# Attention and expert layer on one core: exponential's factor by columns, weight maxima by TensorE, own block for first keys

## Chip, cores and metric

One Trainium2 chip, one of its cores. The time is that of one execution of the program on the device, in microseconds; of several runs the median is given. Profiles are single executions. The program is written for the five engines by hand: TensorE (PE; its weight loads are PEld), VectorE (DVE), ScalarE (ACT), GpSimd (POOL), and SyncE (SP), which issues most DMAs. Each engine works its own queue in order, and they wait for each other on semaphores.

## The reference, cut

```python
x = L0_attn_hidden_states                                   # (4, 1024, 256) f32
x = x + attention(_layernorm(x), Wqa, Wqb, Wkva, Wkvb, Wo)
x = x + experts(_layernorm(x), gate_w, w_gate_up, w_down, shared_gate_up, shared_down)

# attention: 16 heads of 128 (64 plain + 64 rotary), values 128, from a latent of 64
q = ((x @ Wqa) @ Wqb).reshape(b, s, 16, 128)
kv_comp = x @ Wkva;  c_kv, k_pe = kv_comp[..., :64], kv_comp[..., 64:]
q_pe, k_pe = rope(q_pe), rope(k_pe)                         # k_pe is shared by the heads
k_nope, v = split((c_kv @ Wkvb), (64, 128))
scores = einsum('bhqd,bhkd->bhqk', q_full, k_full) * 128 ** -0.5
probs = softmax(where(causal, scores, finfo.min))
out = einsum('bhqk,bhkd->bqhd', probs, v).reshape(b, s, 2048) @ Wo

# experts: top 2 of 16 (softmax of logits), inner size 176, and a shared expert of 352
y = sum over the two chosen e of w_e * (silu(x @ gate_e) * (x @ up_e)) @ down_e
y = y + (silu(x @ g_s) * (x @ u_s)) @ shared_down
```

## The kernel before

**Arithmetic.** Matrices are multiplied in float16 with every operand split into a high and a low part (`hi`, `lo`), three products each. Weights are scaled so that their largest magnitude is `WMAX`. For that `first_weights` takes maxima per partition on VectorE (`largest`, L1336), GpSimd spreads the maxima of the first two columns across partitions with `partition_all_reduce` (L1941; a second one for four more columns at L1978), and `scales` computes the factors. `SPLITS` lists the weights to be split; ScalarE makes the high part (`hi_parts`, L1066), VectorE the low part (`lo_parts`, L1347). The first five entries (`FIRST`) are wanted by the first projections; `wsd` is split at the end of tile 0, `wout`, `wsg` and `wr` in tile 1. K's up-projection is folded into the query weights and V's into the output weights at the start (`wq_made`, `fold_out`), so scores and values work on the latent of 64.

**Tiles.** The 4096 tokens are 32 tiles of 128 (`NT`), eight in a batch (`TB`). Tile t with i = t % 8 has (i+1) x 128 keys. It is worked in units of `GROUP[i]` = 8, 4, 2, 2, 1, 1, 1, 1 heads, so 2, 4, 8, 8, 16, 16, 16, 16 units. For each unit: scores into four banks of PSUM `s_ps` (TensorE), largest score per row (VectorE, `maxima` or `half_maxima`: `smax`), its product with the negative factor `f_natt` (`nmax`, the bias of the exponential), exponential (ScalarE, L1166 and L1171), transposition of the probabilities (TensorE, L853), high part of it (ScalarE, L1039), low part (VectorE, `prob_lo`, L1625), product with the values (TensorE). Scores run two units ahead, exponentials one. `half_maxima` serves tiles with i = 1, 2, 3 (product at L1607) and 6, 7 (L1604); `maxima` serves i = 4, 5 (product at L1585) and i = 0. Between units, at places fixed in the tables `FIRST_TILE` to `LONG`, lie side jobs: projections of tile t+2, output projection of t-1, gates and shared expert of t-2. They share a PSUM bank. GpSimd makes the normalisations (`norm`), the rotation (`rope`; its products are L1885, L1890, L1891), low parts and scatters. From about 1420 us on, the experts' part follows, which the change doesn't touch.

**Order on SP.** Keys and queries of tile n are turned by DMA transposition (`turn_keys`, `turn_queries`, L479, L469) in the section of tile n-2. `kT` holds the keys of one batch; the first two tiles of a batch may be turned into it only when all scores of the batch before are made (L478). `turn_output` turns the outputs; for tile 0 it waits for the split of `wsd`, whose raw weights lie in the buffer `oT`.

**Opening.** TensorE runs `busy` products on a block of ones, then the weight products, `fold_out(0, 1)`, the projections of tiles 0 and 1, the rest of `fold_out`, and `first_scores(0)`. VectorE waits for nine constant tables, converts them, takes the means of the first three tiles of x (each after the normalisation before it, `normed`), then the weight maxima. ScalarE copies the eight pieces of the folded query weights (`wq_copied`) which the eight `amax_q` maxima read.

## Time and profile before

| | us |
|---|---|
| median of 3 runs (lowest, highest) | 1678.92 (1678.5, 1679.54) |
| the profiled execution, its time | 1665.37 |
| its span, first to last instruction | 1663.3 |
| TensorE busy | 1491.1 |
| VectorE busy | 1317.2 |
| ScalarE busy | 1029.8 |
| GpSimd busy | 988.8 |
| mean granted TensorE clock, of full | 0.976 |

Busy times are of one profiled execution. A busy share is a mean over stages with different limits; what ends TensorE's idle time in a stage has to be read from its waits. The profiled execution is shorter than the median of the runs by 13.5 us.

### The profile page before, as it was taken

What the parts mean: (1) busy time and instruction counts of PE and PEld (TensorE: products, weight loads), DVE (VectorE), ACT (ScalarE), POOL (GpSimd) and SP (SyncE); (2) the same over time, 40 slices, a digit from 0 to 9 for tenths busy, and PEclk for the clock granted to TensorE, in tenths of its full rate; (3) what the DMA queues carried; (4) which work ended last, traced back from release to release, by engine and by line L of the source; (5) the groups of instructions that cost most, each with busy time, mean ns of one, the idle gap of its engine ahead of it and who ended that gap; (6) DMA issues with size and microseconds to landing.
All of it is one profiled execution on the core that took longest, in us unless ns stands there. A gap on an engine that the chain in (4) does not pass through costs nothing.

```text
span 1663.3 us, 45076 instructions
## 1 busy us (share of the span) xinstructions
PE 1491.1 (90%) x16403; PEld 1081.6 (65%) x16404; DVE 1317.2 (79%) x2990; ACT 1029.8 (62%) x2342; POOL 988.8 (59%) x1597
## 2 busy tenths in 40 slices
PE   7679999999889999998899999988999998889990
PEld 2356767777666676676667766766677766666660
DVE  2687898887789888887888888878878898565556
ACT  2466666665666666766666666666666676556660
POOL 3267756543687663675878687758686572443440
PEclk9799999999999999999999999999999999999995
DMA  6348832122443312224342223143431211456318
GB/s 188 58 109 191 132 79 55 29 62 57 81 105 75 73 33 60 62 39 94 78 95 60 51 61 65 33 93 82 80 73 42 62 30 35 114 165 201 126 39 306
DMA packets 329879, 144.42 MB, mean 87 GB/s; under 512 B 277347, under 2 KB 320390, under 8 KB 329673
## 3 DMA queue, kind: packets, MB, share of 16 engines
q1 hardware_dynamic: 304592, 105.41, 29.3%
q10 hardware_dynamic: 18168, 19.41, 3.9%
q0 software_dynamic: 6912, 16.83, 3.0%
q8 instruction: 132, 2.16, 0.5%
q14 instruction: 75, 0.61, 0.1%
HBM read 47.04 MB, written 29.53 MB: 46 GB/s over the span
## 4 chain that ended last, share of the span: by engine, by line
PE 53%; DVE 25%; ACT 7%; issue 5%; DMA 4%; SPq 1%; POOL 1%; ACTq 0%; DVEq 0%; POOLq 0%
PE of_ps L683 22%; PE s_ps L683 19%; PE t_ps L853 11%; DVE pT L1625 7%; DVE smax L1596 3%; ACT pT L1039 2%; DVE smax L1600 2%; DVE smax L1578 2%; DVE nmax L1607 2%; DMA qT<-work 1%; ACT work L1039 1%; ACT probs L1171 1%; DVE nmax L1604 1%; DVE work L1430 1%; DVE o_sb L1459 1%
## 5 line engine op out<-in xcount | busy, mean ns | idle before, releaser
L683 PE MATMUL s_ps<-kT,qT 128*128 128x512 f16 (+3 forms) x2304 | 491.4, 328 | 11.3 <-DMA qT<-work 5.5
L1039 ACT CAST pT<-t_ps 128x512 f16<-128x512 f32 (+3 forms) x688 | 354.5, 515 | 236.9 <-PE t_ps L853 235.2
L1625 DVE TENSOR_TENSOR pT<-t_ps,pT 128x512 f16<-128x512 f32 (+3 forms) x688 | 408.8, 597 | 112.3 <-ACT pT L1039 109.5
L853 PE MATMUL t_ps<-id,probs 128*128 128x128 f32 x2304 | 380.3, 280 | 44.6 <-DVE pT L1625 34.5
L853 PEld LDWEIGHTS t_ps<-id,probs 128*128 128x128 f32 x2304 | 255.3, 141 | 143.7 <-issue 97.9
L683 PEld LDWEIGHTS s_ps<-kT,qT 128*128 128x128 f16 x2304 | 218.8, 99 | 78.6 <-DMA qT<-work 6.0
L1166 ACT ACTIVATE probs<-s_ps,nmax,fac 128x640 f32<-128x640 f32 (+3 forms) x256 | 269.0, 1051 | 0.6
L683 PEld LDWEIGHTS of_ps<-ckv,pT 128*128 128x128 f16 x6912 | 241.7, 98 | 40.7 <-DVE o_sb L1459 9.1
L683 PE MATMUL of_ps<-ckv,pT 128*128 128x64 f16 x6912 | 258.4, 193 | 6.7 <-DVE o_sb L1459 6.3
L683 PE MATMUL of_ps<-weights,xT 128*128 128x512 f16 (+1 forms) x936 | 199.9, 350 | 34.7 <-DVE weights L1347 16.4
L1901 POOL TENSOR_TENSOR os_<-o_sb,os_ 128x512 f16<-128x512 f32 x60 | 70.3, 1172 | 162.2 <-ACT os_ L1039 153.3
L1596 DVE TENSOR_REDUCE smax<-s_ps 128x1 f32<-128x512 f32 (+1 forms) x256 | 157.4, 647 | 3.2 <-PE s_ps L683 2.5
L683 PEld LDWEIGHTS of_ps<-weights,xT 128*128 128x128 f16 x936 | 78.5, 99 | 109.8 <-DVE weights L1347 17.1
L1171 ACT ACTIVATE probs<-s_ps,nmax,fac 128x256 f32<-128x256 f32 (+3 forms) x224 | 144.3, 651 | 3.5 <-DVE nmax L1607 3.5
L1578 DVE TENSOR_REDUCE smax<-s_ps 128x1 f32<-128x768 f32 (+2 forms) x136 | 122.6, 901 | 16.2 <-PE s_ps L683 16.1
L683 PE MATMUL s_ps<-maskbf,idbf 128*128 128x128 bf16 x512 | 113.4, 222 | 0.0
L1885 POOL TENSOR_TENSOR work<-work,sin_sb 128x544 f32<-128x544 f32 x60 | 96.4, 1607 | 24.3 <-ACT work L1039 21.7
L1600 DVE TENSOR_REDUCE smax<-s_ps 128x1 f32<-128x512 f32 (+2 forms) x160 | 95.2, 627 | 2.6 <-PE s_ps L683 2.4
L683 PE MATMUL of_ps<-weights,oT 128*128 128x256 f16 x768 | 89.1, 273 | 2.1 <-DVE work L1430 2.1
L683 PE MATMUL s_ps<-wd_sb,work 88*128 (+1 forms) x480 | 72.0, 279 | 17.2 <-DVE work L1773 9.7
L683 PE MATMUL s_ps<-wgu_sb,pT 128*128 (+1 forms) x480 | 86.0, 315 | 0.1
L683 PEld LDWEIGHTS of_ps<-weights,oT 128*128 128x128 f16 x768 | 73.6, 98 | 12.2 <-DVE work L1430 2.5
(227 smaller groups left out, 2434.9 us busy)
## 6 DMA issues: line engine op xcount, KB each, us to landing
wgu_sb<-wgu ACTq DMA_DIRECT2D x8, 704.0 KB, 4.6
work<-lists SPq DMA_DIRECT2D x40, 128.5 KB, 2.2
qT<-lists SPq DMA_DIRECT2D x40, 128.5 KB, 2.2
x_sb<-x SPq DMA_DIRECT2D x32, 128.0 KB, 2.4
x<-x SPq DMA_DIRECT2D x32, 128.0 KB, 2.3
dense<-den SPq DMA_DIRECT2D x32, 128.0 KB, 2.7
weights<-dense ACTq DMA_DIRECT2D x1, 4096.0 KB
qT<-y_exp SPq DMA_DIRECT2D x16, 256.0 KB, 6.9
```

Of the source, the lines that this page charges most:

```text
L683: return pe_.matmul(o, a, b, start=start, stop=stop)
L853: last = pe_.transpose(t_ps[:, h, c * P:(c + 1) * P], probs[:, u % 2, g * L + j * P:g * L + (j + 1) * P], id32[:, :])
L1039: return act.copy(o, i)
L1166: act.activation(probs[:, par, 0:L], s_flat[:, 1024 * par:1024 * par + L], ACT.Exp, bias=nmax[:, par, 0:1], scale=f_att, accum_out=ssum[:, ...
L1171: last = act.activation(probs[:, par, g * L:(g + 1) * L], s_flat[:, base:base + L], ACT.Exp, bias=nmax[:, par, g:g + 1], scale=f_att, accu ...
L1578: dve.tensor_reduce(smax[:, par, 0:G], view, AX_X, ALU.max).then_inc(s.maxs, 1)
L1596: last = dve.tensor_reduce(smax[:, par, h:h + 1], bank[:, 0:(j1 - j0) * P], AX_X, ALU.max)
L1600: last = dve.tensor_reduce(smax[:, par, h * n:(h + 1) * n], view, AX_X, ALU.max)
L1607: last = dve.tensor_scalar(nmax[:, par, 0:G], smax[:, par, 0:G], f_natt, None, ALU.mult)
L1625: dve.tensor_tensor(pT[:, u % 2, 1, h, 0:w], t_ps[:, h, 0:w], pT[:, u % 2, 0, h, 0:w], ALU.subtract).then_inc(s.lo_p, 1)
L1885: st_.do(pool.tensor_tensor(rot2[:, :, k:ROPE:2], pe_of(n)[:, :, 1 - k:ROPE:2], sin_b, ALU.mult))
L1901: pool.tensor_tensor(os_[:, 1, :], o_sb[:, :], os_[:, 0, :], ALU.subtract).then_inc(s.lo_o, 1)
```

## The change

It has these parts. The factor `nmax` is computed for one column per instruction, and where there are two half maxima by a TENSOR_SCALAR with two pointer operands in place of a SCALAR_TENSOR_TENSOR. The first spreading of the weight maxima goes through TensorE: transposition of two columns, maximum over the row, a diagonal of the two values, product with ones. Keys of a batch's first tile get a block of their own, `k0T`; they are turned a second time into `kT` for the later tiles. Identity products (`busy_id`) are put behind the spreading (10) and ahead of the first scores (14). VectorE takes the first mean before the constants, the second and third among the weight maxima. The late splits are cut into six and put behind units of tiles 1 and 2, and the raw `wsd` moves to another buffer.

```diff
--- before.py
+++ after.py
...
+        k0T = sb("k0T", [P, 2, P], F16)
...
+        r_wsd, at = cut(ga, at, 3, D)
...
-        r_wsd, _ = cut(oT[:, :, :, :].rearrange("p a k n -> p (a k n)").bitcast(F32), 0, 3, D)
...
+            *((r_out[:, a:a + 4], wout[:, 0, a:a + 4], wout[:, 1, a:a + 4], P, A_O) for a in (0, 4)),
             (r_wsd, wsd_sb[:, 0], wsd_sb[:, 1], P, A_SD),
-            (r_out, wout[:, 0], wout[:, 1], P, A_O),
-            (r_wsg, wsg_sb[:, 0], wsg_sb[:, 1], P, A_SG),
+            *((r_wsg[:, k], wsg_sb[:, 0, k], wsg_sb[:, 1, k], P, A_SG) for k in range(KD)),
             (r_wr, wr_sb[:, 0], wr_sb[:, 1], P, A_R),
...
+    SPLIT_AT = {at_: slice(FIRST + a, FIRST + b)
+        for at_, (a, b) in {(1, 0): (0, 1), (1, 1): (1, 2), (1, 2): (2, 3), (1, 3): (3, 4), (2, 0): (4, 6)}.items()}
...
             def turn_keys(n):
                 sp.wait_ge(s.rope_done, n + 1)
                 i = n % TB
-                if i < 2 and has(n - 2):
-                    last = n - i - 1
-                    sp.wait_ge(s.s_made, 2 * (unit_of(last, units(last) - 1) + 1))
-                sp.dma_start_transpose(kT[:, :, i * P:(i + 1) * P], ...).then_inc(k_in[n % KS], 16)
+                if i == 0 and has(n - TB):
+                    sp.wait_ge(s.s_made, 2 * unit_of(n - TB + 1, 0))
+                if i == 1 and has(n - 2):
+                    sp.wait_ge(s.s_made, 2 * unit_of(n - 1, 0))
+                dst = kT[:, :, i * P:(i + 1) * P] if i else k0T[:, :, :]
+                sp.dma_start_transpose(dst, ...).then_inc(k_in[n % KS], 16)
+            def turn_first_keys(n):
+                if has(n - 1):
+                    sp.wait_ge(s.s_made, 2 * unit_of(n, 0))
+                sp.dma_start_transpose(kT[:, :, 0:P], ...).then_inc(k0_in, 16)
...
             def turn_output(p, hh):
                 sp.wait_ge(s.lo_o, 2 * p + hh + 1)
-                if p == 0 and hh == 0:
-                    sp.wait_ge(s.lo_made, FIRST + 1)
...
                 if i == TB - 1 and has(t + 1):
                     turn_keys(t + 1)
+                    turn_first_keys(t + 1)
...
             for n in range(2):
                 turn_keys(n)
                 turn_queries(n)
+            turn_first_keys(0)
...
+            def busy_id(o, count):
+                for _ in range(count):
+                    mm(o, id16[:, :], id16[:, :].unsqueeze(1).broadcast_to([P, 4, P]), True, True)
...
                     pe_.wait_ge(k_in[t % KS], 16 * (t // KS + 1))
+                    if i == 1:
+                        pe_.wait_ge(k0_in, 16 * (t // TB + 1))
...
-                                  kT[:, b, c0:c1], a + b == 0, a == 1 and c1 < L)
+                                  kT[:, b, c0:c1] if i else k0T[:, b, c0:c1], a + b == 0, a == 1 and c1 < L)
...
             fold_out(0, 1)
+            pe_.wait_ge(s.amax_ready, 1)
+            pe_.transpose(f_ps[0:2, 0:P], amax[:, 0:2], id32[:, :]).then_inc(s.amax_turned, 1)
+            pe_.wait_ge(s.amax_spread, 1)
+            mm(f_ps[:, P:P + 2], ones_r[:, :], diag_w[:, :], True, True).then_inc(s.amax_turned, 1)
+            busy_id(s_ps[:, 1, :], 10)
...
             fold_out(1, H // 4)
+            busy_id(s_ps[:, 3, :], 14)
             first_scores(0)
...
+                if (t, k) == (2, 0):
+                    act.wait_ge(s.lo_made, FIRST + 3)
...
                     if (t, k) == (1, 0):
-                        hi_parts(SPLITS[FIRST + 1:FIRST + 2])
-                    if (t, k) == (1, 1):
-                        hi_parts(SPLITS[FIRST + 2:])
+                        act.wait_ge(s.scales, 2)
+                    if (t, k) in SPLIT_AT:
+                        hi_parts(SPLITS[SPLIT_AT[t, k]])
                     expert_loads(t, k)
                 side(t, units(t), 0)
-                if t == 0:
-                    act.wait_ge(s.scales, 2)
-                    hi_parts(SPLITS[FIRST:FIRST + 1])
...
                 for n in range(8):
+                    if n in (1, 4):
+                        means(1 if n == 1 else 2, -1)
                     dve.wait_ge(s.wq_copied, n + 1)
...
-                dve.wait_ge(s.amax_reduced, 1)
-                scales(slice(0, 2))
+                dve.wait_ge(s.amax_turned, 1)
+                link(dve.tensor_reduce(top_w[:, :], f_ps[0:2, 0:P], AX_X, ALU.max))
+                dve.tensor_scalar(diag_w[:, :], id32[0:2, 0:2], top_w[:, 0:1], None, ALU.mult).then_inc(s.amax_spread, 1)
+                dve.wait_ge(s.amax_turned, 2)
+                scales(slice(0, 2), f_ps[:, P:P + 2])
...
                 if G == 1:
-                    last = dve.scalar_tensor_tensor(nmax[:, par, 0:1], smax[:, par, 0:1], smax[:, par, 1:2], f_natt, ALU.max,
-                                                    ALU.mult)
+                    last = dve.tensor_scalar(nmax[:, par, 0:1], smax[:, par, 0:1], smax[:, par, 1:2], f_natt, ALU.max, ALU.mult)
                 else:
-                    last = dve.tensor_scalar(nmax[:, par, 0:G], smax[:, par, 0:G], f_natt, None, ALU.mult)
+                    for g in range(G):
+                        last = dve.tensor_scalar(nmax[:, par, g:g + 1], smax[:, par, g:g + 1], f_natt, None, ALU.mult)
...
             means(0, -1)
-            means(1, -1)
-            means(2, -1)
+            constants()
             first_weights()
...
-                    if (t, k) == (1, 0):
-                        lo_parts(FIRST + 1, FIRST + 2)
-                    if (t, k) == (1, 1):
-                        lo_parts(FIRST + 2, len(SPLITS))
+                    if (t, k) in SPLIT_AT:
+                        lo_parts(SPLIT_AT[t, k].start, SPLIT_AT[t, k].stop)
...
-                if t == 0:
-                    lo_parts(FIRST, FIRST + 1)
...
-            pool.wait_ge(s.amax_ready, 1)
-            pool.partition_all_reduce(amax_all[:, 0:2], amax[:, 0:2], P, bass.bass_isa.ReduceOp.max).then_inc(s.amax_reduced, 1)
```

## Rows read from the trace of the kernel before

**Rows 1.** Page, busy time of TensorE and VectorE with share of the span
```profile
PE 1491.1 (90%) x16403; PEld 1081.6 (65%) x16404; DVE 1317.2 (79%) x2990; ACT 1029.8 (62%) x2342; POOL 988.8 (59%) x1597
```

**Rows 2.** Waits of TensorE, 125 to 1420 us: total us, times, longest us
```profile
PE t_ps L853 <- DVE pT L1625: 31.4, 63, 1.5
...
PE s_ps L683 <- DMA kT<-ks_sb: 5.0, 3, 2.2
```

**Rows 3.** VectorE's groups by form: count | busy us, mean ns | idle before
```profile
L1604 DVE SCALAR_TENSOR_TENSOR nmax<-smax,fac 128x1 f32<-128x1 f32 x128 | 49.6, 387 | 4.5
L1607 DVE TENSOR_SCALAR nmax<-smax,fac 128x2 f32<-128x2 f32 x64 | 44.0, 687 | 2.3
L1585 DVE TENSOR_SCALAR nmax<-smax,fac 128x1 f32<-128x1 f32 x128 | 27.4, 214 | 4.5
```

**Rows 4.** Timeline 479 to 484 (tile 10): start us, us, engine, instruction [idle before]
```profile
480.11 2.49 POOL L1891 TENSOR_TENSOR work<-work 128x1088 f32<-128x1088 f32 x1
...
480.29 2.34 DVE L1607 TENSOR_SCALAR nmax<-smax,fac 128x2 f32<-128x2 f32 x1
...
483.23 0.52 PE L853 MATMUL t_ps<-id,probs 128*128 128x128 f32 x3 [1.49 <-DVE pT L1625]
```

**Rows 5.** Timeline 257 to 260 (tile 5), GpSimd and VectorE
```profile
258.27 2.50 POOL L1891 TENSOR_TENSOR work<-work 128x1088 f32<-128x1088 f32 x1
...
258.39 0.21 DVE L1585 TENSOR_SCALAR nmax<-smax,fac 128x1 f32<-128x1 f32 x1
```

**Rows 6.** Timeline 79 to 81, VectorE, two independent small instructions
```profile
80.02 0.14 DVE L1385 TENSOR_SCALAR fac<-wamp 128x1 f32<-128x1 f32 x1
80.08 0.20 DVE L1386 TENSOR_SCALAR fac<-wamp 128x1 f32<-128x1 f32 x1
```

**Rows 7.** Timeline of the opening, all engines (SPq issues DMAs)
```profile
25.25 0.43 DVE L1479 BATCH_NORM_STATS2 ln_st<-x_sb 128x6 f32<-128x256 f32 x1 [6.55 <-POOLq L675]
...
33.17 0.27 DVE L1354 MEMSET oT<- 32x256 f32 x1
...
36.29 4.83 DVE L1336 TENSOR_REDUCE amax_q<-work 128x1 f32<-128x512 f32 x8
...
45.74 0.17 DVE L1339 TENSOR_SCALAR amax_all<-amax_all 128x2 f32<-128x2 f32 x1 [4.37 <-POOL amax_all L1941]
...
49.59 2.74 PE L683 MATMUL of_ps<-weights,xT 128*128 128x512 f16 x6 [1.02 <-DVE weights L1347]
...
71.36 0.50 PE L683 MATMUL s_ps<-kT,qT 128*128 128x128 f16 x3 [5.52 <-DMA qT<-work]
...
72.67 4.97 SPq L469 DMA_TRANSPOSE qT<-pT  x1
...
74.13 0.39 POOL L1978 PARTITION_ALL_REDUCE amax_all<-amax  x1 [8.16 <-DVEq L1379]
```

**Rows 8.** DMA issues at the start, and issues by tensor: KB each, us to landing
```profile
4.37 1.06 SPq L417 DMA_DIRECT2D x_sb<-x  x2
...
11.14 0.46 ACTq L1043 DMA_DIRECT2D wd_sb<-gateT  x1
...
x_sb<-x SPq DMA_DIRECT2D x3, 128.0 KB, 9.4
...
wd_sb<-gateT ACTq DMA_DIRECT2D x1, 16.0 KB, 12.3
```

**Rows 9.** Windows: us, busy (instructions) of PE, PEld, DVE, ACT, POOL, PEclk, DMA share, GB/s
```profile
47.00:51.00 4.00, 2.24 (x10) 1.15 (x11) 3.24 (x4) 4.00 (x5) 0.00 (x0) 0.50 0.01 2
...
406.00:410.00 4.00, 4.00 (x52) 3.93 (x51) 1.71 (x2) 0.58 (x1) 0.00 (x0) 0.59 1.10 250
```

**Rows 10.** Timeline, VectorE and TensorE, end of tile 0 and first scores of tile 8
```profile
97.89 1.84 DVE L1347 SCALAR_TENSOR_TENSOR weights<-oT,winv,weights 128x768 f16<-128x768 f32 x1
...
100.48 1.08 PE L853 MATMUL t_ps<-id,probs 128*128 128x128 f32 x4 [3.10 <-DVE pT L1625]
...
404.76 0.33 PE L683 MATMUL s_ps<-kT,qT 128*128 128x128 f16 x3 [2.23 <-DMA kT<-ks_sb]
```

More of the change, by code:

```diff
@@ L1325, in _, with constants @@
-            dve.tensor_scalar(first_e[:, :], iota_e_sb[:, :], float(LIST), None, ALU.mult)
-            dve.memset(ones_e[:, :], 1.0)
-            dve.memset(amax_e[:, :], 0.0)
-            link(dve.memset(amax[:, :], 0.0))
-            dve.tensor_scalar(used[:, :], iota_e_sb[:, :], float(LIST), None, ALU.mult)
-            dve.sem_inc(s.c_ready, 1)
-            dve.sem_inc(s.m_y, 1)
+            def constants():
+                dve.wait_ge(s.c_in, 16 * 9)
+                dve.tensor_copy(id16[:, :], id32[:, :])
+                dve.tensor_copy(idbf[:, :], id32[:, :])
+                dve.tensor_copy(maskbf[:, :], probs[:, 1, 0:P])
+                dve.tensor_copy(tri16[:, :], probs[:, 0, 0:P])
+                dve.memset(ones16[:, :], 1.0)
+                dve.memset(ones_r[:, :], 1.0)
+                dve.memset(hs[:, :, :], 0.0)
+                dve.tensor_scalar(iota_k_sb[:, :], iota_k_sb[:, :], float(P - 1), None, ALU.add)
+                dve.tensor_scalar(first_e[:, :], iota_e_sb[:, :], float(LIST), None, ALU.mult)
+                dve.memset(ones_e[:, :], 1.0)
+                dve.memset(amax_e[:, :], 0.0)
+                link(dve.memset(amax[:, :], 0.0))
+                dve.tensor_scalar(used[:, :], iota_e_sb[:, :], float(LIST), None, ALU.mult)
+                dve.sem_inc(s.c_ready, 1)
+                dve.sem_inc(s.m_y, 1)
@@ L1335, in largest, with scales @@
             def largest(o, src):
                 return dve.tensor_reduce(o, src, AX_X, ALU.max, apply_absolute_value=True)
-            def scales(cols):
-                link(dve.tensor_scalar(amax_all[:, cols], amax_all[:, cols], 1e-30, None, ALU.max))
+            def scales(cols, largest_=None):
+                src = amax_all[:, cols] if largest_ is None else largest_
+                link(dve.tensor_scalar(amax_all[:, cols], src, 1e-30, None, ALU.max))
                 link(dve.tensor_scalar(wamp[:, cols], amax_all[:, cols], 1.0 / WMAX, None, ALU.mult))
```

28 lines of the change are left out of this document (13 added, 15 removed).

## The prediction

> **What bounds the kernel now.** I read the page's busy shares first: TensorE is busy for 1491 of 1663 us and VectorE for 1317 [rows 1], so a gain must come out of the 172 us in which TensorE is idle. The waits of TensorE between 125 and 1420 us come next, the stretch of the 32 attention tiles after the first two: 31.4 us of idle time, in 63 pieces, lie before its transposes of the probabilities and end with VectorE's low parts (L1625); 5.0 us, in three pieces, end with the turned keys of a new batch [rows 2]. The rest is small or not touched. Then VectorE's groups by form: the little product that makes the exponential's bias, `nmax`, takes 387 ns as SCALAR_TENSOR_TENSOR of one column (L1604), 687 ns as TENSOR_SCALAR of two columns (L1607), and 214 ns as TENSOR_SCALAR of one column (L1585) [rows 3]. The same arithmetic should not cost three times as much. The timeline shows why: at 480.29 the product lasts 2.34 us, until GpSimd's multiplication that had begun at 480.11 is over; the next low parts start only then, and TensorE stands idle for 1.49 us [rows 4]. A one-column TENSOR_SCALAR, begun 0.12 us after a GpSimd instruction of 2.50 us of the same kind, takes its 0.21 us [rows 5]. Last, the timeline, DMA landings and clock of the opening [rows 7 to 9].
>
> **Part A, the factor one column at a time.** Excess over 214 ns: 128 x (387-214) = 22 us at L1604, 64 x (687-214) = 30 us at L1607, together 52 us of VectorE time. The one-column pair costs one more issue: independent TENSOR_SCALARs stand 0.06 us apart [rows 6], so 64 x 0.06 and, for four columns, 16 x 0.18 go back: 7 us, leaving 45 us of VectorE time. What reaches TensorE is less. I went through its 31.4 us of waits: about 20 us of them, in 33 pieces, come within 4 us of an `nmax` product of over 0.3 us ([rows 2, 4] show the sum and one of the largest). The others follow long reductions and stay. Small waits of ScalarE on the same product would go too. I take -19 us; floor -10, if half of that idle time is only handed on to the next releaser; ceiling -28, if excess that I did not see as a wait also counts. No row shows a TENSOR_SCALAR of one column with two pointer operands (the new L1604 form). Its nearest row is L1585 at 214 ns, from above the old form at 387; I take L1585's, and the gain of L1604's 22 us of excess is what hangs on it.
> The Trainium skill's "DVE: scalar operands, raw-bit mode, write accounting and state across instructions", section "Scalar operands", says that a pointer scalar doesn't take up the second tensor stream, which speaks for that choice; no run here shows it yet.
> Against the change speaks the Trainium skill's "VectorE: DVE Perf Modes", section on the TRN2 errata: many small instructions each pay a fixed term of about 150 cycles. As an estimate from that page, 112 more instructions would take some 17 us of VectorE instead of my 7, and part A would be about 4 us smaller; the 0.06 us between two of them in the trace [rows 6] speaks against it.
>
> **Part B, a block of its own for the first keys.** Before, the keys of a batch's first tile may be turned into `kT` only when all scores of the batch before are made; TensorE then waits 2.23 us at 404.76 [rows 10], 5.0 us over the three boundaries [rows 2]. At the first the clock falls too: 0.59 of full between 406 and 410 us [rows 9], and 4 us of work at that rate could be done in 2.4, so 1.6 us more. With `k0T` the transposition is issued long before, its wait (scores of the batch's tile 0) being long over. The copy of the same keys into `kT` takes the old place in SP's queue, ahead of `turn_keys` and `turn_queries` of the next tile, so those land when they did. The wait on it is put on the first scores of tile 1, several us later, and costs nothing as long as TensorE gains less than those. Gain 5.0 to 6.6; next is the exponential's chain of the new batch, which starts as much earlier. I take -5.5, between -3 and -7.
>
> **Part C, the opening up to the first scores.** (1) Before, the first mean came behind the constants on VectorE. Now it goes first: x is issued at 4.37 and lands 9.4 us later [rows 8], 13.8. A normalisation on GpSimd takes 6.55 us (the idle time before 25.25, [rows 7]), so the first is over at 21.0. (2) The weight maxima start when the last weights land, 11.14 + 12.3 = 23.4 [rows 8], instead of at 33.17. Up to the eight `amax_q` reductions 3.1 us (33.17 to 36.29), one reduction 0.6 (4.83/8): 27.2. The second mean (0.65) and its normalisation: 34.4; before the fifth reduction VectorE waits for this. Third mean 0.65, four reductions 2.4, two closing ones 0.3: 37.8, where before it was 36.29+4.83+0.3 = 41.4 [rows 7]. Gain 3.6. (3) The all-reduce on GpSimd kept VectorE waiting 4.37 us [rows 7]. In its place stand a transposition, a reduction over two partitions, a product, and a matmul: no rows for these shapes; four small operations at 0.15 to 0.45 us with their hand-overs, 1.5 us, within 0.8 and 3. Gain 2.9. (4) Ten identity products are queued after it. TensorE has idled and the clock is at 0.50 in 47 to 51 [rows 9], where a 512-wide product takes 2.74/6 = 0.46 us [rows 7]: they end at 39.2 + 4.6 = 43.8, while the first projection could start 2.0 us after the scales, at 41.3. That costs 2.5; it gives back up to 3.9, as three groups of six products ran at 2.74 instead of about half of it. Net some 7 us at the end of the rotary columns of tile 0, then the chain to the turned queries is unchanged: first scores at 64.4 instead of 71.36. Fourteen more identity products (3.0 us at full clock, 6.4 at half) fit into the 5.5 us that TensorE waits there. (5) On SP `turn_first_keys(0)` comes behind the 4.97 us issue of tile 1's queries [rows 7]; tile 1's scores wait for it: +1 us. Together -6.5, between -2 (clock stays down and the products only delay) and -9. (6) The second all-reduce, now the first on GpSimd, may take the 4 us that the first needed, while the second started 0.2 us after its data [rows 7]. VectorE reaches the scales behind two maxima and a mean, some 4.5 us later: hidden, at worst +1.
> (7) The splits. `wsd`'s low part (1.84 us) is gone from the end of tile 0, where TensorE waits 3.10 us for VectorE at 100.48 [rows 10]; the work is as much, in smaller pieces over four units of tile 1 and one of tile 2. SP's wait of `turn_output` on that split goes too, ScalarE's new one before the second half's loads finds its split done two units before. TensorE's clock also fell behind that wait. I take -3.5: 1.8 directly and 1.7 of clock and of the lumps of tile 1; bounds 0 and -6.
>
> **Sum.** -19 -5.5 -6.5 -3.5 = -34.5 us. The profiled execution spans 1663.3 and took 1665.4, so it should come to about 1631; the median of the runs is 1678.9, 13.5 above it. I carry that distance over unchanged: 1644.4.
>
> **Rivals.** *TensorE takes over in part A*: VectorE's saved 45 us turn into idle time, since TensorE waits otherwise for ScalarE's high parts or its own queue. For it: only 20 of 52 us of excess are visible as waits. Against: these waits end with L1625 directly behind the product. Part A then gives -9: 1654.
> *The opening doesn't pay*: the identity products run at 1.2 GHz and delay the projections while the clock rises no sooner, the code of the all-reduce arrives late on the path. Part C(1 to 6) gives -1 instead: 1650.
> *The one-column form waits as well* (the slower side, and the case that the change doesn't do what it says). Then L1607 has two waits for one: 64 x 0.459 = 29 us more on VectorE. It makes the kernel slower only if over half of that reaches TensorE (15.5/29); if all does, 1678.9 + 29 - 15.5 = 1692. Against it stand the 128 one-column products of L1585, mean 214 [rows 3, 5].
>
> **Chances.** Forecast 0.60 (own range 1634 to 1654), TensorE takes over 0.20, opening doesn't pay 0.13, one-column waits 0.04, and 0.03 for gains that cancel against something unseen. The range for 8 in 10 takes in the first three and the bounds of A: 1631 to 1661. Measurements of this kernel tell about 0.2% (3.4 us) from no change: faster 0.93, within 0.03, slower 0.04.
>
> **What would show it.** Right: every `nmax` product near 0.21 us whatever GpSimd does, the waits on L1625 in 125 to 1420 down from 31 to some 13 us, no wait for keys at batch starts, first scores near 64 us, clock full before the first rotary columns end. Wrong: `nmax` of one column still at 0.4 us or more; waits of the same sum under ScalarE's name; first scores later than 68; a clock at half during the projections.

## The result: 1660.1 us instead of 1679.6, and the profile after

The changed kernel takes 1660.05 us (median of 8 runs, 1653.18 to 1672.3), the kernel before beside it 1679.57 (1678.5 to 1684.35): a ratio of 0.987, interval [0.985, 0.9889], so 19.5 us less. The forecast was 34.5 us less, 1644.4. The direction held. The wide range, 1631 to 1661, held by 1 us only, and so by luck as much as by insight: 1660 lies outside the forecast's own range (1634 to 1654) and above both rivals that still gain (1654 and 1650). Every term of the sum came out smaller than forecast.

The profiled execution of the kernel before that the prediction reads was 14 us shorter than its median, the one of the changed kernel (1661.34) is an ordinary one, and so the kernel before was profiled once more (run e5 below, span 1681.6). Where tiles or waits are compared here, it is with that profile. In the experiments below two executions were far above the rest (2162 us in e1, 3915 us in e2): they count in the medians of the table, which without them are 1658.6 and 1667.0, but not in the ratios.

The changed kernel, first the page (busy us, share of the span), then the waits of TensorE between 120 and 1400 us (total us, times, longest), which answer to [rows 1, 2]:

```profile
span 1659.5 us, 45247 instructions
...
PE 1497.1 (90%) x16430; PEld 1087.0 (66%) x16431; DVE 1289.5 (78%) x3107; ACT 1028.4 (62%) x2344; POOL 990.3 (60%) x1596
...
PE t_ps L872 <- DVE pT L1661: 17.2, 38, 1.2
PE t_ps L872 <- ACT probs L1193: 9.7, 25, 1.1
PE of_ps L698 <- ACT work L1064: 8.1, 14, 1.3
PE of_ps L698 <- DVE work L1466: 7.6, 13, 2.3
PE of_ps L698 <- DVE ks_sb L1453: 4.2, 7, 1.0
...
PE s_ps L698 <- DMA qT<-work: 2.5, 2, 1.8
```

The waits on VectorE's low parts (now L1661) are down to 17.2 us, those for the keys of a batch are gone, and there is a new one: 2.5 us for turned queries. The groups of `nmax` on VectorE (count | busy us, mean ns | idle before) and, under them, the durations in ns (min/median/max) of the two-pointer form, which answer to [rows 3]:

```profile
L1640 DVE TENSOR_SCALAR nmax<-smax,fac 128x1 f32<-128x1 f32 x128 | 34.9, 273 | 4.7
L1643 DVE TENSOR_SCALAR nmax<-smax,fac 128x1 f32<-128x1 f32 x192 | 30.6, 208 | 2.8
...
L1640 DVE TENSOR_SCALAR nmax<-smax,fac x128: 272/273/276, 286.1 to 1391.7; 128x1 f32<-128x1 f32 x128
L1643 DVE TENSOR_SCALAR nmax<-smax,fac x192: 202/205/216, 76.5 to 1185.3; 128x1 f32<-128x1 f32 x192
```

No `nmax` product waits for GpSimd any more: 211 of the 320 begin while an instruction of GpSimd is under way, and none is longer than 276 ns. In e5, of the 208 that the change touches, 77 take over 300 ns, and 72 of these end within 0.15 us of the end of a GpSimd instruction that had begun before them. But the form with two pointer operands is not 214 ns long but 273.

### The profile page after: what moved, and what is told of

The parts are those of the page before. It is cut to its first block, busy times and chain, and to the rows that moved or that the text cites. A ratio compares the mean times of both kernels' runs of the same rounds, so it can differ in the third digit from the quotient of the medians.

```text
span 1659.5 us, 45247 instructions
## 1 busy us (share of the span) xinstructions
PE 1497.1 (90%) x16430; PEld 1087.0 (66%) x16431; DVE 1289.5 (78%) x3107; ACT 1028.4 (62%) x2344; POOL 990.3 (60%) x1596
## 4 chain that ended last, share of the span: by engine, by line
PE 60%; DVE 17%; ACT 7%; issue 5%; DMA 4%; SPq 2%; POOL 1%; another core or an unknown queue 0%; ACTq 0%; DVEq 0%; POOLq 0%
PE of_ps L698 25%; PE s_ps L698 21%; PE t_ps L872 13%; DVE pT L1661 5%; DVE smax L1632 2%; ACT pT L1064 2%; DMA qT<-work 2%; DVE smax L1614 1%; ACT work L1064 1%; ACT probs L1193 1%; ACT probs L1198 1%; DVE o_sb L1495 1%; DVE smax L1636 1%; DMA work<-y_exp 1%; PE of_ps L980 1%
## 5 line engine op out<-in xcount | busy, mean ns | idle before, releaser
L1661 DVE TENSOR_TENSOR pT<-t_ps,pT 128x512 f16<-128x512 f32 (+3 forms) x688 | 409.2, 598 | 133.7 <-ACT pT L1064 127.0
L698 PE MATMUL s_ps<-kT,qT 128*128 128x512 f16 (+3 forms) x2112 | 474.7, 337 | 4.5 <-DMA qT<-work 4.5
L872 PE MATMUL t_ps<-id,probs 128*128 128x128 f32 x2304 | 381.3, 280 | 34.6 <-DVE pT L1661 17.2
L698 PEld LDWEIGHTS of_ps<-ckv,pT 128*128 128x128 f16 x6912 | 241.0, 98 | 41.9 <-DVE o_sb L1495 10.1
L698 PEld LDWEIGHTS s_ps<-kT,qT 128*128 128x128 f16 x2112 | 203.7, 98 | 71.3 <-DMA qT<-work 5.2
L1614 DVE TENSOR_REDUCE smax<-s_ps 128x1 f32<-128x768 f32 (+2 forms) x136 | 122.6, 902 | 10.6 <-PE s_ps L698 10.2
```

Source lines behind the costliest of these rows:

```text
L698: return pe_.matmul(o, a, b, start=start, stop=stop)
L872: last = pe_.transpose(t_ps[:, h, c * P:(c + 1) * P], probs[:, u % 2, g * L + j * P:g * L + (j + 1) * P], id32[:, :])
L1614: dve.tensor_reduce(smax[:, par, 0:G], view, AX_X, ALU.max).then_inc(s.maxs, 1)
L1661: dve.tensor_tensor(pT[:, u % 2, 1, h, 0:w], t_ps[:, h, 0:w], pT[:, u % 2, 0, h, 0:w], ALU.subtract).then_inc(s.lo_p, 1)
```

## Experiments

e1 to e8 ran on one chip, e9 to e11 on a second and e12 on a third, each beside runs of the kernel before; the medians of these are 1682.3 us (e1 to e4), 1682.6 (e5 to e8), 1683.7 (e9 to e11) and 1681.1 (e12). Ratios are the measure. In us (the ratio times the median of the kernel before), with half the interval's width, they are:

```
run                          median   ratio [95%]              us against before
e1  the change               1659.6   0.9868 [0.9851, 0.9885]  -22.2 +- 2.9
e2  part A alone             1667.3   0.9909 [0.9895, 0.9924]  -15.3 +- 2.4
e3  opening alone            1678.6   0.9979 [0.9966, 0.9992]   -3.5 +- 2.2
e4  part B alone             1681.7   0.9992 [0.9983, 1.0002]   -1.3 +- 1.6
e5  before, once more        1683.3   1.0004 [0.9991, 1.0018]   +0.7 +- 2.3
e6  all but A                1678.2   0.9973 [0.9960, 0.9987]   -4.5 +- 2.3
e7  all but B                1663.7   0.9898 [0.9864, 0.9933]  -17.2 +- 5.8
e8  no identity products     1663.0   0.9903 [0.9871, 0.9936]  -16.3 +- 5.5
e9  all but the splits       1661.2   0.9863 [0.9840, 0.9886]  -23.1 +- 3.9
e10 first keys by a copy     1661.6   0.9872 [0.9850, 0.9894]  -21.6 +- 3.7
e11 two-pointer form alone   1676.2   0.9958 [0.9944, 0.9972]   -7.1 +- 2.4
e12 copy, batches 2 to 4     1658.4   0.9871 [0.9853, 0.9889]  -21.7 +- 3.0
```

**e1, the change, and e5, the kernel before, once more.** No edit in either.

> The changed kernel once more, unaltered, as the measure for its neighbours and to see what of its profile returns. In its first profile ScalarE stood still twice for 3.0 and 3.8 us near 1440 us, for a releaser that the profile can't name, where the kernel before has no such wait. Theory 'chance': these stalls move or are gone in this profile, the experts' part lasts about 253 us as before, and the span is near 1650. Theory 'the change causes them': they stand at the same place again, and the experts' part lasts 262 us. Time expected: 1660, 0.987 of before, by both.

> The kernel before, profiled once more. Its profiled execution took 1665.4 us where the median of its runs is 1679.6, so all comparisons of its trace with others are off by some 14 us. Theory 1 (the profiled execution of before was an uncommonly short one): now near 1680 (ratio 1.000), and the 14 us more show where e1 to e4 have them as well: about 9 us of ScalarE waits that the profile puts down to 'remote' in the experts' part between 1435 and 1480 us, waits of TensorE for the exponentials of 640 to 1024 columns (0.6 to 1.5 us in each tile with i = 4 or 5). Rival (these waits came with the change): the new profile looks like the old one, with none of them, and the changed kernel really loses some 14 us there.

The change is confirmed at -22 us. In e1 ScalarE stands still at the same places again (3.0 and 3.8 us, at 1438 and 1443 us) and the experts' part lasts 262.1 us: that is what e1's second theory said, that the change causes the stalls, and e5 has to decide whether the kernel before has them too. The new profile of the kernel before spans 1681.6 us; here are TensorE's waits in it, 125 to 1420 us, and two of ScalarE's idle spells in the experts' part (start us, us, engine, instruction, [idle before]):

```profile
PE t_ps L853 <- DVE pT L1625: 33.1, 61, 1.4
PE of_ps L683 <- ACT work L1039: 9.9, 15, 1.3
PE t_ps L853 <- ACT probs L1166: 9.1, 25, 1.1
PE of_ps L683 <- DVE work L1430: 6.5, 13, 1.5
PE s_ps L683 <- DMA kT<-ks_sb: 5.4, 3, 2.7
...
1462.67 0.41 ACT L1249 ACTIVATE work<-s_ps,fac 128x176 f32<-128x176 f32 x1 [3.06 <-issue]
...
1489.60 0.41 ACT L1249 ACTIVATE work<-s_ps,fac 128x176 f32<-128x176 f32 x1 [3.35 <-remote]
```

The 9.1 us of waits for the exponentials (`probs` L1166) and ScalarE's idle spells with no releaser stand in the kernel before as well, so the 9.7 us under the same name in the changed kernel are not handed on from part A, as one would say from the first profile. e5's theory 1 holds. The two terms on which the sum rests read much the same in both profiles: 33.1 against 31.4 us for L1625, 5.4 against 5.0 for the keys.

Durations by tile show the stages. A tile's start is taken 0.6 us before ScalarE's first high parts of its probabilities; i is the tile's number in its batch. Between two executions of one kernel a tile can differ by more than a microsecond with no edit near it: the changed kernel's first profile has 35.4 us in tile 2, where e1 has 32.9. These are worked out from the timelines, in us:

```
                          e5     e2     e11    e6     e7     e9     e12    e1
start of tile 0           80.1   80.7   79.8   73.6   72.0   72.9   73.8   72.1
tile 1                    28.8   29.3   30.5   33.5   32.9   29.0   31.3   31.5
tile 2                    32.6   32.2   32.6   36.3   34.3   37.1   31.8   32.9
start of tile 3          159.7  160.2  160.8  160.5  156.0  157.3  154.3  153.8
tile 7  (i = 7)           68.5   66.9   66.8   64.2   65.7   64.2   64.2   64.2
tile 8  (i = 0)           20.8   20.9   20.8   21.4   20.9   21.8   21.0   21.5
tile 10 (i = 2)           34.4   32.7   34.4   34.4   32.7   32.7   32.8   32.7
tile 11 (i = 3)           37.3   34.9   37.3   37.2   34.9   34.9   34.9   34.9
tile 12 (i = 4)           46.2   46.1   46.1   46.4   46.1   46.1   46.1   46.1
tile 14 (i = 6)           56.9   55.3   55.3   56.9   55.3   55.3   55.3   55.3
tile 15 (i = 7)           65.6   65.7   65.8   64.1   65.7   64.2   64.2   64.2
tile 16 (i = 0)           20.9   20.9   20.9   22.6   20.9   23.0   21.3   22.7
tiles 8 to 31           1003.3  990.3  998.2 1006.4  990.2  989.8  988.0  988.9
```

**e2, part A alone; e11, half of it; e6, all the rest.** The edit of e2, of which e11 makes only the first half and e6 undoes both:

```diff
-last = dve.scalar_tensor_tensor(nmax[:, par, 0:1], smax[:, par, 0:1], smax[:, par, 1:2], f_natt, ALU.max, ALU.mult)
+last = dve.tensor_scalar(nmax[:, par, 0:1], smax[:, par, 0:1], smax[:, par, 1:2], f_natt, ALU.max, ALU.mult)
...
-last = dve.tensor_scalar(nmax[:, par, 0:G], smax[:, par, 0:G], f_natt, None, ALU.mult)
+for g in range(G):
+    last = dve.tensor_scalar(nmax[:, par, g:g + 1], smax[:, par, g:g + 1], f_natt, None, ALU.mult)
```

> The kernel before with part A alone: nmax one column per instruction. Theory 'price as forecast': the waits of TensorE on the low parts fall from 31 to 17 us, -14 to -19 us (1661 to 1666). Theory 'handed on': tiles 4 and 5, which the edit doesn't touch, get slower by some 0.8 us each as in the changed kernel's profile (4 us in all), waits on ScalarE's exponentials take over, and the gain is 8 to 11 us (1669 to 1672).

> The changed kernel with part A undone (nmax by scalar_tensor_tensor, and two and four columns in one instruction). By the experiments so far part A is worth 15 us alone; if the parts add up, this takes 1659.6 + 15 = 1675 us (ratio 0.9955). If part A's gain also feeds on the others (its waits vanish elsewhere), 1670 or less; by the forecast's terms (A = 19) 1679.

> The kernel before with only the first half of part A: the product of tiles with one head a unit (i = 4 to 7) by tensor_scalar with two pointer operands in place of scalar_tensor_tensor. It took 387 ns before and takes 273 in the changed kernel, so 128 x 0.114 = 14.6 us of VectorE time go; the other half frees 64 x 0.65 + 16 x 0.27 - 192 x 0.208 = 6 us by mean durations alone. If the gain follows freed VectorE time, this half carries 15 x 14.6 / 20.6 = 10.6 us: 1672 (ratio 0.9937). If it follows the waits of TensorE instead (by tiles, e2_columns_only against the kernel before once more: tiles i = 2 and 3 shorter by 9.3 us in all, i = 6 and 7 by 4.5), it is the smaller half: 4 to 6 us, 1677 to 1679 (0.997).

Part A is worth 15.3 us alone and 17.7 +- 3.7 in the whole change (e6 against e1); the two agree within the noise, so the parts add up as far as can be seen, and 19 isn't excluded for the whole. Waits of TensorE, 125 to 1420 us, in e2 and then in e11:

```profile
PE t_ps L853 <- DVE pT L1625: 16.0, 37, 1.2
PE of_ps L683 <- ACT work L1039: 11.5, 16, 1.5
...
PE of_ps L683 <- DVE o_sb L1459: 4.5, 8, 0.9
PE of_ps L683 <- DVE ks_sb L1417: 3.8, 7, 1.0
```
```profile
PE t_ps L853 <- DVE pT L1624: 26.7, 49, 1.4
```

The waits on the low parts go from 33.1 (e5) to 26.7 with the two-pointer form alone and to 16.0 with both: 6.4 and 10.7 us, and the times fall by 7.1 and 8.2 more. So the gain did not follow the freed VectorE time, by which e11 was to bring 10.6 us, but the waits; the 4 to 6 us that e11's other theory took from the tiles lie within the interval of 7.1 +- 2.4. The table shows where: over tiles 8 to 31 the tiles with i = 2 and 3 lose 10.1 us by the one-column pieces, those with i = 6 5.1 us by the two-pointer form, and those with i = 7, whose products were changed just as much, nothing. The tiles with i = 4 and 5 don't change either, but the edit doesn't touch them: `maxima` serves them, and the words "i = 4 to 7" in e11's expectation should be i = 6 and 7. Three other waits grow by 4.3 us in e2 (`work` of ScalarE 9.9 to 11.5, `o_sb` 3.7 to 4.5, `ks_sb` 1.9 to 3.8), for one of 1.6 us (for `x2T`) that goes: 2.7 us net come back under other names. All waits of this view together fall from 79.3 us in e5 to 65.2 in e2 over the same tiles (125 to 1405 us in e2), so by 14.1, close to the 15.3 of the times.

**e3, the opening alone; e8, the change without its identity products.** e3 has the reordered means and constants, the spreading by TensorE and both groups of identity products, with the keys, the splits and `nmax` as before. e8:

```diff
-            busy_id(s_ps[:, 1, :], 10)
...
-            busy_id(s_ps[:, 3, :], 14)
```

> The kernel before with the opening alone: spreading by TensorE, identity products, order of the means; splits, keys and nmax as before. Theory 'forecast': first unit of tile 0 starts 7 us earlier and stays so: -6 to -7 us (1673). Theory 'given back': the transposed queries of tiles 2 and 3 collide with the expert weight loads whatever comes before, and tiles 1 and 2 give back 4 to 5 of the 7 us: -2 us (1677.5).

> The changed kernel without the 24 identity products that run ahead of the first projection and ahead of the first scores. If they pay (the clock is full before the rotary columns end), the clock stays at half for some 20 us from 36 us on instead of 10, first scores come 3 to 5 us later and the time is 1663 to 1665. If they only delay (the rival 'the opening doesn't pay': they hold TensorE for 4.1 us at half clock, over 3 of it in front of the first projection), it is the same or 1 to 2 us faster: 1657 to 1660.

The opening of the changed kernel (timeline; answers to [rows 7]):

```profile
38.15 0.28 DVE L1400 TENSOR_REDUCE top_w<-of_ps 2x1 f32<-2x128 f32 x1 [0.52 <-PE of_ps L930]
38.47 0.22 DVE L1401 TENSOR_SCALAR diag_w<-id,top_w 2x2 f32<-2x2 f32 x1
...
39.36 0.16 DVE L1369 TENSOR_SCALAR amax_all<-of_ps 128x2 f32<-128x2 f32 x1 [0.68 <-PE of_ps L698]
...
43.17 1.79 PE L698 MATMUL of_ps<-weights,xT 128*128 128x128 f16 x12
...
64.16 0.50 PE L698 MATMUL s_ps<-k0T,qT 128*128 128x128 f16 x3 [3.58 <-DMA qT<-work]
...
65.72 0.39 POOL L2007 PARTITION_ALL_REDUCE amax_all<-amax  x1 [8.15 <-DVEq L1415]
```

And 36 to 57 us in windows (busy us and instructions of PE, PEld, DVE, ACT, POOL, then TensorE's granted clock, DMA share, GB/s), the changed kernel and then e5:

```profile
36.00:43.00 7.00, 4.63 (x13) 1.96 (x14) 5.06 (x14) 2.73 (x4) 4.40 (x14) 0.51 0.14 33
43.00:50.00 7.00, 7.00 (x43) 3.57 (x42) 5.34 (x8) 4.62 (x10) 2.86 (x2) 1.00 0.06 12
```
```profile
43.00:50.00 7.00, 0.82 (x6) 0.56 (x6) 2.08 (x7) 2.30 (x3) 0.37 (x1) 0.50 0.00 1
50.00:57.00 7.00, 6.38 (x19) 2.48 (x20) 4.58 (x6) 3.74 (x7) 0.45 (x1) 0.61 0.01 2
```

The maxima are complete at 37.6 us (forecast 37.8), the spreading takes 1.7 us (1.5), the first projection starts at 43.2 (43.8), the first scores at 64.2 (64.4). The projections run at the full clock, where in e5 they started at half of it. In e8 the first projection starts at 42.45 and runs at half clock, and the clock is full again from 50 us on. First scores come 1.2 us later than in e1 (66.16 against 64.92), where 3 to 5 were expected, and 0.6 of that was there before the products (the spreading's last product starts at 39.37 against 38.80). Tile 0 starts 1.9 us later, and the run takes 3.4 us more by the medians of the table, 5.9 +- 6.2 by the ratios. So the identity products cost nothing that shows and give back some 0.7 us up to the first scores; that the run gains by them is likely, not shown. The rival "the opening doesn't pay", worth -1 us, is answered by e3, and narrowly: -3.5 +- 2.2. The all-reduce on GpSimd, now the first of its kind, starts 0.2 us after its data, so no cost of a first use was moved onto the second scales.

What does not arrive is all of the gain behind it: tile 0 starts 8.0 us earlier in e1 than in e5, tile 3 5.9 (in e3: 7.3 and 4.5). Tiles 1 and 2 take the difference back. In the changed kernel's first profile (TensorE in tile 1; then SP, ScalarE and TensorE in tile 2):

```profile
101.99 0.66 PE L698 MATMUL s_ps<-kT,qT 128*128 128x384 f16 x3 [1.99 <-DMA qT<-work]
105.76 2.45 PE L698 MATMUL of_ps<-weights,oT 128*128 128x256 f16 x21 [2.06 <-DMA oT<-os_]
...
122.88 6.44 SPq L476 DMA_TRANSPOSE qT<-work  x1
...
132.86 0.59 ACT L1064 CAST work<-of_ps 128x512 f16<-128x512 f32 x1 [3.45 <-DMA qT<-work]
...
134.22 2.02 PE L698 MATMUL of_ps<-weights,xT 128*128 128x512 f16 x6 [2.27 <-DVE work L1466]
```

The transposition of the queries, whose issue alone holds SP for 6.44 us (5.04 in e5 at the same place), reads `work`; ScalarE may write `work` again only when it has landed, and TensorE waits for that. The wait of ScalarE in tile 2 is not new: it is 2.7 us in e5, 1.4 in e1 and 4.3 in e3 and e9, and tile 2 takes 32.6 us in e5, 32.9 in e1, 35.6 in e3 and 37.1 in e9. What is new is in tile 1: TensorE waits 2.6 us for queries and 1.8 for turned outputs in e1, 3.0 and 1.4 in e3. Those queries (of tile 2) land 8.2 us after their issue in e1 and 8.5 in e3, but 5.6 in e5; part B's experiments, below, show that this difference comes with the opening. In e5 tile 1 has no wait for a DMA; its two largest are 3.1 us for the low parts, which stood behind the large split, and 2.8 us for `x`. This is read from the rows; no run took the transposition away.

A second place takes some of the opening's gain. In e3 tile 31 starts 7.3 us earlier than in e5 (2.8 of this in tile 7, where the wait for keys is shorter, 1.4 us, and the clock doesn't fall), but from there to the end it takes 1.8 us longer. TensorE stands idle there once, some 107 us after the start of tile 31, for 8.0 to 8.7 us in every profile with the new opening (e1, e3, e6 to e10, e12) and for 3.7 to 4.1 in those with the old one (e2, e4, e5, e11), and nowhere as long in the first profile of the kernel before. So this wait comes with the opening; by what way, no run shows.

**e9, all but the splits.** One large piece at the end of tile 0 and two lumps in tile 1 again:

```diff
-        SPLIT_AT = {at_: slice(FIRST + a, FIRST + b)
-                    for at_, (a, b) in {(1, 0): (0, 1), (1, 1): (1, 2), (1, 2): (2, 3), (1, 3): (3, 4), (2, 0): (4, 6)}.items()}
...
+                if t == 0:
+                    lo_parts(FIRST, FIRST + 1)
```

> The changed kernel with the splits of the weights and their landing place as before (one large piece at the end of tile 0, the rest in two lumps of tile 1). By the forecast's term the new arrangement is worth 3.5: 1663 us (ratio 0.989). The product of the three parts alone leaves 2 us for it: 1661.5 (0.988). Rival (the pieces only move the waits): in the profiles tile 1 is longer with the new pieces (31.2 to 33.5 us) than with the old ones (28.8 to 30.5); if that cancels what tile 0 and the clock give, the time is the changed kernel's, 1659 to 1660.5 (0.987).

0.9863 against 0.9868: the new arrangement is worth nothing that shows (difference -0.8 +- 4.9 us, so a gain of up to some 4 us isn't excluded). In the profiles tile 1 is 2.4 us shorter with the old splits and tile 2 4.3 longer. The forecast's wait of 3.1 us behind the large piece [rows 10] did go, and waits for queries and turned outputs took its place.

**e4, part B alone; e7, all but B; e10 and e12, the first keys by a copy.**

> The kernel before with the block of its own for first keys alone. Theory 'forecast': no wait for kT at 404, 744 and 1079 us, -5 to -6 us (1674). Theory 'handed on': the wait moves to the queries of the next tile (in the changed kernel's profile 0.7 and 1.8 us of waits on qT stand in tiles 8 and 16, where none stood), -2 to -3 us (1677).

> The changed kernel with part B undone: the first keys of a batch go into kT again and wait for the old batch's last scores. By the forecast's term +5.5: 1665 us (ratio 0.990). By e4_first_keys_only (part B alone -1): 1660.5 (0.987). If the turned queries, which wait in tiles 8 and 16 of the changed kernel (0.7 and 1.8 us), are late because part B puts one more transposition ahead of them, then those waits are gone here and part B costs as much as it gives: 1659 to 1661; a wait for keys of 1.3 to 2.6 us stands at 405, 740 and 1074 us again.

> The changed kernel, but the first keys come into kT by a copy of 128x256 fp16 on VectorE at the start of a batch's first tile, in place of the third DMA transposition at that point of SP's queue (1.2 to 2.6 us of issue each, ahead of the queries of the tile after). Theory (part B gave part of its 1.5 us a boundary back, because that transposition holds up the next queries): TensorE's waits for queries in tiles 8 and 16 (0.7 and 2.0 us) go, the copy costs some 0.2 us of VectorE four times, and the time falls by 2 to 3 us: 1657 to 1658 (ratio 0.985). Rival (the queries land as late for another reason, their own issue of 4.7 to 5.0 us): waits and time stay, 1659 to 1660.5.

> As e10_first_keys_by_copy, but the first batch keeps its transposition; the copy on VectorE serves the second to fourth batch only. In e10 the waits for queries in tiles 8 and 16 were gone (tile 8 took 20.97 instead of 21.47, tile 16 21.23 instead of 22.73), tile 24 was 0.3 longer, and tile 0 took 20.7 instead of 17.4 us, because the copy stood behind the second scales on VectorE and the scores of tile 1 waited 2.2 us for it. If that is all, tile 0 is back near 17 us and the sum over tiles 8 to 31 stays 2 us below the changed kernel's (986.8 against 988.9): 1657 to 1658 us (ratio 0.9855). If the gain of e10's later tiles is taken up elsewhere, the sum is 988 to 989 again and the time 1659.6 (0.9868).

e10 takes the second transposition of the first keys out of SP's queue and copies them on VectorE, at the start of each batch's first tile; e12 does so from the second batch on.

```diff
-            def turn_first_keys(n):
-
-                if has(n - 1):
-                    sp.wait_ge(s.s_made, 2 * unit_of(n, 0))
-                sp.dma_start_transpose(kT[:, :, 0:P], ks_sb[:, n % KS].rearrange("p s d -> p (s d)")).then_inc(k0_in, 16)
...
+            def copy_first_keys(t):
+                dve.wait_ge(k_in[t % KS], 16 * (t // KS + 1))
+                dve.wait_ge(s.s_made, 2 * unit_of(t, 0))
+                dve.tensor_copy(kT[:, :, 0:P], k0T[:, :, :]).then_inc(k0_in, 1)
```

The boundary before tile 16: in e7 (without B) TensorE waits for the keys; in e1 it does not, SP issues three transpositions in a row, and TensorE waits some 6 us later for the queries of tile 17; in e12 the copy replaces one of the three and that wait is gone.

```profile
736.26 0.33 PE L685 MATMUL s_ps<-kT,qT 128*128 128x128 f16 x3 [1.31 <-DMA kT<-ks_sb]
```
```profile
730.18 1.17 SPq L495 DMA_TRANSPOSE kT<-ks_sb  x1
731.45 2.59 SPq L489 DMA_TRANSPOSE kT<-ks_sb  x1
734.21 5.02 SPq L476 DMA_TRANSPOSE qT<-work  x1
...
742.48 0.50 PE L698 MATMUL s_ps<-kT,qT 128*128 128x256 f16 x3 [1.96 <-DMA qT<-work]
```
```profile
730.46 1.17 SPq L490 DMA_TRANSPOSE kT<-ks_sb  x1
731.80 6.01 SPq L476 DMA_TRANSPOSE qT<-work  x1
...
740.93 0.21 DVE L1764 COPY kT<-k0T 128x256 f16<-128x256 f16 x1
741.28 0.49 PE L695 MATMUL s_ps<-kT,qT 128*128 128x256 f16 x3 [0.53 <-DVE kT L1764]
```

Neither expectation of e4 holds as it stands: the waits for keys are gone, no wait for queries took their place, and still the time falls by 1.3 +- 1.6 us only. By the tiles of e7 and e1, B takes 1.5 us out of each last tile of a batch (65.7 to 64.2, three times, 4.5 in all) and puts 0.6 and 1.8 us into tiles 8 and 16: 2.1 us net. The times say -1.3 +- 1.6 (e4) and -5.0 +- 6.5 (e7 against e1). e10 and e12 show that without the additional transposition the waits for queries don't arise: the waits for the queries of tiles 9 and 17 go (tile 8 takes 21.0 instead of 21.5, tile 16 21.3 instead of 22.7). But in e10 the copy stood behind the second scales on VectorE and held up the scores of tile 1 by 2.2 us, and in e12, which avoids that, the sum over tiles 8 to 31 is 988.0 against 988.9, where 986.8 was expected; tiles 9, 20, 24 and 25 are 0.3 to 0.4 us longer. Its time, 0.9871 against 0.9868, does not differ from the change's. No version tried is measurably faster than the changed kernel.

But the additional transposition doesn't make a wait by itself. In e4 it stands at the same place, TensorE wants the queries as much earlier, and it waits at none of the three boundaries; nor does it in e8 before tile 17. The same boundary in e4:

```profile
745.73 1.17 SPq L490 DMA_TRANSPOSE kT<-ks_sb  x1
747.00 1.20 SPq L484 DMA_TRANSPOSE kT<-ks_sb  x1
748.36 4.16 SPq L471 DMA_TRANSPOSE qT<-work  x1
```

One difference runs through all profiles. The same transposition of the queries holds SP longer with the new opening than with the old one. Its 31 issues (min/median/max in ns, first and last start) in e4 (part B alone), e3 (opening alone) and e1:

```profile
L471 SPq DMA_TRANSPOSE qT<-work x31: 3947/4029/8780, 66.8 to 1302.9; - x31
L472 SPq DMA_TRANSPOSE qT<-work x31: 4720/4880/6125, 58.9 to 1298.6; - x31
L476 SPq DMA_TRANSPOSE qT<-work x31: 4723/4867/7606, 58.2 to 1281.2; - x31
```

The median is 4.0 to 4.1 us in the kernel before, e2, e4, e5 and e11, and 4.8 to 5.0 in all that have the new opening (e1, e3, e6 to e10, e12). The queries of tile 0 land 5.5 us after their issue in e4 and e5 and 6.7 us in e1, e3, e6, e8 and e12. The opening thus makes every transposition of queries longer, in the whole kernel, and e4 doesn't pay for it. Which of its edits does so no run shows. It is neither the identity products, which e8 leaves out, nor part B or the splits. A candidate is that three small buffers (`ones_r`, `top_w`, `diag_w`) were put ahead of `work` and `qT` and may have moved them; putting them behind would settle it.

Before tile 17 a second thing is added in e1: the queries are issued 4.0 us after the first of the transpositions, where it is 2.6 in e4 and e7, because the middle one holds SP for 2.59 us and not 1.20. What makes that one longer in e1, e6 and e9 is open. In e4 tiles 7, 15 and 23 are 4.3, 1.5 and 1.5 us shorter than in e5 and tiles 8, 16 and 24 as long as before; tiles 1, 14 and 21, in which TensorE waits for no DMA, are 1.7, 1.1 and 1.0 longer. Why so little of the 7.3 us reaches the end is open.

The fall of the clock before tile 8 is not tied to the length of the wait either. e5 waits 2.70 us there and the clock falls, e2 waits 2.60 us and it stays full (windows as above, e5 and then e2):

```profile
407.00:411.00 4.00, 3.57 (x35) 3.54 (x36) 0.00 (x0) 0.59 (x1) 0.00 (x0) 0.57 0.86 197
```
```profile
405.00:410.00 5.00, 4.45 (x80) 4.28 (x80) 2.01 (x2) 1.17 (x2) 0.00 (x0) 1.00 0.92 209
```

Tile 7 takes 68.5 us in e5 and 66.9 in e2, with waits of nearly the same length, so the fall costs some 1.6 us where it happens, as the forecast had it.

## Why the forecast was right in direction and 15 us too large

**Part A, -19 forecast, -15.3 alone (-17.7 in the whole).** The mechanism is the one named: no product waits for GpSimd any more, and the waits on L1625 fell from 33.1 to 17.2 us (31 to some 13 was forecast). The term in the sum was the 20 us of TensorE's waits near an `nmax`, nearly all of it taken as gain. 17.1 us of the waits on L1625 went (e2), and 2.7 us came back under other names. The VectorE time behind it was mis-sized more: 45 us freed in the forecast, 24.8 measured (busy time 1314.2 in e5, 1289.4 in e2). The two-pointer form costs 273 ns and not L1585's 214: 128 x 0.059 = 7.6 us. And a further small instruction costs more than the 0.06 us of [rows 6]: two pieces of `nmax` take 0.34 us together where one takes 0.205, so the second adds 0.135, and 112 of them 15 us instead of 7. The mean of L1607 is also 649 ns in e5, not 687, which is 2.4 us more. The pair:

```profile
135.13 0.34 DVE L1643 TENSOR_SCALAR nmax<-smax,fac 128x1 f32<-128x1 f32 x2
```

Here the rule that the prediction set aside was the better one: the Trainium skill's "VectorE: DVE Perf Modes", section on the TRN2 errata, puts a fixed term of about 150 cycles on every small instruction (0.156 us at that page's 0.96 GHz, an estimate), and the prediction's estimate of 17 us from it is closer to the 15 measured than its own 7. That part A also came out smaller by 4, as that estimate said, is in part chance: the longer two-pointer form and the waits that came back have their share in it. The rival "TensorE takes over" (-9) was the right kind of loss in too large a size; "the one-column form waits as well" is refuted, with 276 ns as the longest of 320.

The lock itself is seen in the spread of e5's durations (min/median/max in ns):

```profile
L1604 DVE SCALAR_TENSOR_TENSOR nmax<-smax,fac x128: 219/220/1749, 291.6 to 1415.9; 128x1 f32<-128x1 f32 x128
L1607 DVE TENSOR_SCALAR nmax<-smax,fac x80: 228/244/2260, 84.9 to 1208.4; 128x2 f32<-128x2 f32 x64, 128x4 f32<-128x4 f32 x16
```

The means of 387 and 687 ns [rows 3] are those of many short instructions and some very long ones: 77 of the 208 take over 300 ns, 24 over 1000. The Trainium skill's "SBUF — State Buffer", section "Who interferes with whom", says that VectorE and GpSimd share one pair of ports, that a VectorE instruction with two inputs in SBUF or in a two-port mode needs it, and that the later of the two stands until the other's instruction is over. These maxima, the 72 long products that end together with a GpSimd instruction, and the absence of long ones in the one-column forms agree.

**Part B, -5.5 forecast, some -2 by the tiles, -1.3 +- 1.6 alone.** The waits for keys went as said. The step that failed in the whole change is "so those land when they did": before tile 17 the queries are issued 4.0 us after the first transposition and not 2.6, and TensorE wants them 1.5 us sooner. That TensorE wants them sooner is not enough by itself, since e4 has no such wait. With the new opening each transposition of queries also holds SP 0.8 us longer, which the forecast, for part B and for the opening, put at nothing. That this makes the waits fits all profiles, but no run took it away. The further 1.6 us of clock belong to the one fall of the clock at 406 [rows 9]. It comes in some executions and not in others: e2 waits 2.60 us there and e7 1.31 with the clock full, so in the whole change this gain was not B's to make. The waits to be saved were smaller there too, 3.9 us in e7 for the 5.0 of [rows 2]. Why part B alone gives 1.3 us and not 4 or more is open.

**Part C (1 to 6), -6.5 forecast, -3.5 +- 2.2.** Each time of the chain held within 0.6 us, up to first scores at 64.2 where 64.4 was forecast. That this last one fits is in part chance: "the chain to the turned queries is unchanged" is wrong by the 1.2 us that they land later. What failed is the step from there to the end of the kernel: that tile 0's gain stays whole. The next two tiles take 2 to 4 us of it, where TensorE waits for what SP's queue transposes, more slowly than before for the queries, and the longer idle spell in the experts' part, which comes with the new opening, up to 2 more. The price of the ten identity products was too high in the forecast (some 1.3 to 1.7 us and not 2.5: the first projection starts 4.4 us after the spreading's last product in the changed kernel, 4.8 in e1 and 3.1 in e8), and so was what they give back: the projections and the rest of `fold_out` take 17.0 us in e8 and 14.6 in e1, so 2.4, where up to 3.9 was forecast.

**Part C (7), -3.5 forecast, nothing that shows.** The wait behind the split went and was replaced in the same tile by waits for queries and turned outputs. As in B, the wait was counted as gain without the next one behind it. e9 leaves up to some 4 us open.

**The sum.** The parts measured alone give -20.1, the whole -22.2 in the experiments and -19.5 in the first comparison. Carrying the 13.5 us between the profile and the median over unchanged was not the error: e5, an ordinary execution, gives the same two wait sums. The experts' part was not expected to change; it is 1.4 us longer in e1 than in e5 (262.1 against 260.7), with TensorE idle for 8.7 us in one place where e5 has 4.1. Of the 14.4 us between the forecast and the parts measured alone, part A has 3.7, B 4.2, C (1 to 6) 3.0 and C (7), by e9, all of its 3.5, each with the interval given above.

## What to carry to other kernels

Look at the median and the maximum of a small instruction, not only at its mean: a median of 220 ns and a maximum of 1749 say that it waits, and a one-column form of the same arithmetic may not. When waits of one releaser are removed, look up the next releaser in each of the places (here 2.7 of 17.1 us came back), and where the work is fed through an ordered DMA queue, check when the next transfer in that queue is needed on the new schedule before counting the gain of an earlier one. Compare the durations of instructions that the edit doesn't touch, too: here one transposition became 0.8 us longer in the whole kernel. Don't count a fall of the clock as saved from one profile: of four profiles of this case with a wait of over 2 us at the same place, two have it (the first one of the kernel before, e5) and two don't (e2, e11). A gain in the opening has to be followed through the first tiles until two profiles run in step.

## What the runs showed of the hardware that was not expected

A one-column TENSOR_SCALAR with two pointer operands takes 272 to 276 ns, with one 202 to 216 ns. A copy of 128x256 fp16 on VectorE took 0.21 to 0.23 us in all seven cases in e10 and e12, where the issue of the transposition that it replaces holds SP for 1.17 us. And two executions of one unchanged kernel differ by 18 us in their spans (1663.3 and 1681.6): ScalarE has three idle spells of 2.1 to 3.4 us with the releaser "issue" or "remote" in the longer one and none in the other, and TensorE waits 9.1 us instead of 2.7 for the exponentials of 640 and more columns. What holds ScalarE there no run shows.
